# Local attention: TensorE's step put in the order of its tile shapes, one more step of pipeline depth, the token shift moved to ScalarE

## What is computed

```
for i in range(6):
    x = attn_layer(shift_tokens(x), Wqkv[i], ...) + x    # 16 heads of 64, windows of 32 tokens,
                                                         # each sees itself and the window before
    x = ffn_layer(shift_tokens(x), ...) + x              # layer norm, gated GELU, 341 hidden
shift_tokens(t): the upper half of the channels comes from the token before
attn_layer: q, k normalised per head (l2), rotary tables with a scale, scores * 8, causal mask, softmax, @ v, @ Wo
```

## Time and profile before

| | us |
|---|---|
| median of 3 runs (4217.25 to 4219.12) | 4217.94 |
| the profiled execution | 4230.46 |
| its span, first to last instruction | 4228.0 |
| one layer of local attention, first projection to first projection (1326.78 to 1905.23) | 578.45 |
| of it, end of the last step begun and MLP (1805.67 to 1905.23) | 99.56 |
| a step in the steady part | 7.605 |

### The profile page before, as it was taken

One profiled execution on the slowest core, in us unless ns is written; L12 is line 12 of the kernel. 1 busy time (PEld: TensorE's weight loads), 2 busy tenths in 40 slices (PEclk: granted clock), 3 DMA queues, 4 the chain that ended last, 5 costly groups with the idle time before them and its releaser, 6 DMA issues. The chain is left out here.

```text
span 4228.0 us, 154817 instructions
## 1 busy us (share of the span) xinstructions
PE 3986.5 (94%) x61339; PEld 2359.9 (56%) x61339; DVE 3368.7 (80%) x5724; ACT 2583.2 (61%) x5027; POOL 2537.1 (60%) x2772
## 2 busy tenths in 40 slices
PE   5888697999999999999999999999999999999998
PEld 3555486555554555545555545555455555455554
DVE  5777455899976999958999769999489997699994
ACT  4776222566665666665666656666666666566665
POOL 2111133777763777727777537777277775477771
PEclk8999998999999999999999999999999999999999
DMA  2000000000000000000000000000000000000001
GB/s 72 0 0 1 0 0 3 3 0 0 0 21 7 0 0 0 0 21 6 0 0 0 21 6 0 0 0 0 21 6 0 0 0 21 6 0 0 0 0 41
DMA packets 12340, 27.26 MB, mean 6 GB/s; under 512 B 2460, under 2 KB 6728, under 8 KB 11344
## 3 DMA queue, kind: packets, MB, share of 16 engines
q1 hardware_dynamic: 12240, 25.72, 1.7%
HBM read 23.62 MB, written 2.10 MB: 6 GB/s over the span
## 5 line engine op out<-in xcount | busy, mean ns | idle before, releaser
L954 POOL TENSOR_TENSOR w_t<-w_t 128x512 f32<-128x512 f32 x768 | 981.2, 1278 | 509.0 <-DVE w_t L1259 508.8
L1259 DVE TENSOR_TENSOR w_t<-banks,w_tab 128x512 f32<-128x512 f32 x1536 | 981.6, 681 | 46.1 <-PE banks L1130 27.7
L989 POOL TENSOR_TENSOR w_t<-w_t,w_rn 128x512 f32<-128x512 f32 x768 | 784.9, 1043 | 243.1 <-ACT w_rn L1434 243.1
L1069 PE MATMUL banks<-w_vo,w_xs 128*32 128x256 f32 x12288 | 823.2, 385 | 8.6 <-ACT w_us L1382 8.6
L1130 PE MATMUL banks<-w_qk,w_xs 128*128 128x512 f32 x1536 | 767.2, 622 | 5.8 <-issue 4.1
L1069 PEld LDWEIGHTS banks<-w_vo,w_xs 128*32 128x32 f32 x12288 | 321.7, 109 | 499.8 <-issue 368.6
L1393 ACT ACTIVATE w_pr<-w_pr 128x512 f32<-128x512 f32 x384 | 242.0, 630 | 581.8 <-DVE w_pr L1306 581.8
L1382 ACT ACTIVATE w_us<-banks 128x512 f32<-128x512 f32 x768 | 457.3, 596 | 173.1 <-PE banks L1069 173.1
L1288 DVE TENSOR_REDUCE w_ss<-w_sq 128x16 f32<-128x1024 f32 x384 | 464.3, 1209 | 0.0
L1108 PE MATMUL banks<-w_us,w_prT 128*32 128x128 f32 x10752 | 418.3, 276 | 20.7 <-issue 9.4
L981 POOL TENSOR_TENSOR w_pr<-w_pr,w_rl 128x512 f32<-128x512 f32 x384 | 403.1, 1050 | 35.0 <-DVE w_rl L1274 35.0
(11 more groups left out here) (176 smaller groups left out, 5838.2 us busy)
## 6 DMA issues: line engine op xcount, KB each, us to landing
w_qk<-w_qk_in SPq DMA_DIRECT2D x7, 1024.0 KB, 4.8
w_v<-w_v_in SPq DMA_DIRECT2D x7, 512.0 KB, 5.5
w_o<-w_o_in SPq DMA_DIRECT2D x7, 512.0 KB, 6.3
m_w<-m_w_in SPq DMA_DIRECT2D x6, 342.0 KB
xT<-x_in SPq DMA_DIRECT2D x4, 512.0 KB
out<-kept SPq DMA_DIRECT2D x8, 256.0 KB, 2.4
m_w<-m_w_in SPq DMA_DIRECT2D x6, 171.0 KB
r_tab<-r_tab_in SPq DMA_DIRECT2D x1, 512.0 KB
```

The source lines that it names most:

```text
L954: nc.gpsimd.tensor_tensor(v1, v1, v2[:, :, ::-1, :], ALU.add).then_inc(S["added"], 1)
L989: nc.gpsimd.tensor_tensor(v1, v1, rn[j % 2][:, i * HALF:(i + 1) * HALF].unsqueeze(2) .broadcast_to([P, HALF, WD]), ALU.mult).then_inc(S["n ...
L1069: last = nc.tensor.matmul(banks[WIN * g:WIN * (g + 1), 2, lo:lo + 2 * P], x[:, WIN * w:WIN * (w + 1)], wvo[:, first:first + 2, :].rearrang ...
L1259: nc.vector.tensor_tensor(dst[j % 2][:, i * C:(i + 1) * C].rearrange("p (h d) -> p h d", d=WD), src, tab[:, 2 * t + cs, i * WD:(i + 1) * W ...
```

## The change

- PE's step has a new order: projection of k, turn of q (tile n-1), projection of q, turn of k (n-1), in every second step the turned output, turn of the probabilities (now tile n-3), first half of the values, weighted values (now n-3), second half of the values, scores (n-1). All of 128*128 stand together, then all of 128*32, then the scores.
- The tile's way is one step longer: mask, maximum and subtraction are made for tile n-2 at the head of DVE's step, turn of the probabilities and weighted values for tile n-3; `LAG` is 4.
- DVE's order is: mask, maximum, subtraction (n-2); rotation of k; rotation of q; residual; sums of the squares and guard; sum of the exponentials (n-2) and reciprocal.
- ACT's order is: shift of x (new, in every second step, two copies of 64x128); square of k; copy of turned q (n-1); square of q; copy of turned k (n-1); copy of the turned probabilities (n-3); first half of the values; exponential (n-2); copy of the output; second half of the values; the two activations of the inverse norm.
- POOL's order is: edge copy (now for the tile n-2); addition for k; addition for q; multiplication by the inverse norm, twice; probabilities (n-2) times the reciprocal. It has no shift of x any more; the shifts of the first two MLP chunks are ACT's too.

The diff, cut to its core; what is left out takes away the same work from its old place or gives helpers their names:

```diff
--- before.py
+++ after.py
@@ -826,7 +826,7 @@
-    LAG = 3
+    LAG = 4
...
@@ -953,34 +941,14 @@
...
+                    if live(2) and j2 < 2:
+                        pool.wait_ge(S["u_taken"], passed(n(2) * 2))
+                        if live(4):
+                            pool.wait_ge(S["valued"], passed(n(4)))
                         pool.sem_inc(sem("gate"), 1)
+                        nc.gpsimd.tensor_copy(edge[j2][:], us[j2][:, NWIN - 1]).then_inc(S["edged"], 1)
                     if live(0):
                         add(1, "k_rotated")
...
-                    if live(2):
-                        pool.wait_ge(S["inverse"], passed(n(2)))
-                        p = pr[j % 2]
-                        nc.gpsimd.tensor_tensor(p[:], p[:], rl[j % 2][:].unsqueeze(1).unsqueeze(3)
-                                                .broadcast_to([P, 2, HALF, WIN]), ALU.mult).then_inc(S["weighted"], 1)
-                    if live(0):
                         add(0, "q_rotated")
...
@@ -988,10 +956,12 @@
...
+                    if live(2):
+                        pool.wait_ge(S["inverse"], passed(n(2)))
+                        p = pr[j % 2]
+                        nc.gpsimd.tensor_tensor(p[:], p[:], rl[j % 2][:].unsqueeze(1).unsqueeze(3)
+                                                .broadcast_to([P, 2, HALF, WIN]), ALU.mult).then_inc(S["weighted"], 1)
...
@@ -1075,21 +1061,21 @@
...
-                        pe.wait_ge(S["weighted"], passed(n(2)))
+                        pe.wait_ge(S["weighted"], passed(n(3)))
...
-                        tv, hv = j2 // 2, j2 % 2
-                        pe.wait_ge(S["p_taken"], passed(n(2)))
-                        pe.wait_ge(S["u_taken"], passed(n(2) * 2))
+                        tv, hv = j3 // 2, j3 % 2
+                        pe.wait_ge(S["p_taken"], passed(n(3)))
+                        pe.wait_ge(S["u_taken"], passed(n(3) * 2))
...
@@ -1177,13 +1116,59 @@
...
+                    if live(0):
+                        if live(1):
+                            pe.wait_ge(S["k_rotated"], passed((n(0) - 1) * 2))
...
+                        project(1)
...
+                    if live(1):
+                        if live(4):
+                            pe.wait_ge(S["p_taken"], passed(n(4)))
+                        elif not live(2):
+                            pe.wait_ge(M["residual"], finished(layer, 0))
+                        turn(0)
+                    if live(0):
+                        if live(1):
+                            pe.wait_ge(S["q_rotated"], passed((n(0) - 1) * 2))
+                        pe.sem_inc(sem("gate"), 1)
+                        project(0)
+                    if live(1):
+                        turn(1)
...
+                    if live(4) and j % 2 == 1:
+                        pe.wait_ge(S["y_taken"], passed(tiles(layer, j, seq, 4)))
+                        pe.sem_inc(sem("gate"), 1)
+                        nc.tensor.transpose(banks[:, 7, P:2 * P], ysb[:], ident[:]).then_inc(S["y_turned"], 1)
+                    if live(3):
+                        turn_probabilities()
...
+                    if live(0):
+                        values(0)
+                    if live(3):
+                        apply_probabilities()
+                    if live(0):
+                        values(1)
...
+                    if live(1):
+                        scores()
...
@@ -1261,59 +1245,56 @@
+                    if live(2):
+                        dve.wait_ge(S["scored"], passed(n(2)))
...
+                            dve.wait_ge(S["p_turned"], passed(n(4)))
...
-                        dve.wait_ge(S["qk"], passed(n(0) * 2 - 1))
+                        dve.wait_ge(S["k_squared"], passed(n(0)))
                         if live(2):
                             dve.wait_ge(S["turned"], passed(n(2) * 2))
                         rotate(1, "k_rotated")
+                        dve.wait_ge(S["q_squared"], passed(n(0)))
+                        rotate(0, "q_rotated")
...
+                    if live(4) and j % 2 == 1:
+                        dve.wait_ge(S["y_turned"], passed(tiles(layer, j, seq, 4)))
+                        lo = PAD + (j // 2) * P
+                        rows = xT[:, bass.ds(seq - 1, 1), lo:lo + P].rearrange("p b t -> p (b t)")
+                        nc.vector.tensor_tensor(rows, rows, banks[:, 7, P:2 * P], ALU.add).then_inc(S["residual"], 1)
+                    if live(0):
+                        nc.vector.tensor_reduce(ss[j % 2][:], sq[:].rearrange("p a h d -> p (a h) d"), AX, ALU.add)\
+                            .then_inc(S["sums"], 1)
+                        dve.wait_ge(S["sums"], passed(n(0)))
+                        nc.vector.tensor_scalar(ss[j % 2][:], ss[j % 2][:], 1e-24, None, ALU.max)\
+                            .then_inc(S["guarded"], 1)
                     if live(2):
                         dve.wait_ge(S["exped"], passed(n(2)))
...
@@ -1371,6 +1352,20 @@
+                def shift(t, seq):
+                    src = xT[:, bass.ds(seq, 1), :].rearrange("p b t -> p (b t)")
+                    lo = PAD + t * P
+                    for rows, back in ((slice(0, 64), 0), (slice(64, P), 1)):
+                        nc.scalar.activation(xs[t][rows, :], src[rows, lo - back:lo - back + P], ACT.Copy)\
+                            .then_inc(S[f"shifted{t}"], 1)
+
+                def shift_chunk(c):
+                    act.wait_ge(S["residual"], passed(layer * B * TILES + 2 * TILES * (c + 1)))
+                    for rows, back in ((slice(0, 64), 0), (slice(64, P), 1)):
+                        nc.scalar.activation(xm[c][rows, :].rearrange("p (b t) -> p b t", b=PER),
+                                             xT[rows, c * PER:(c + 1) * PER, PAD - back:PAD - back + T], ACT.Copy)\
+                            .then_inc(M["early"], 1)
...
@@ -1382,57 +1377,72 @@
...
+                    if live(0) and j % 2 == 0:
+                        if live(1):
+                            act.wait_ge(S["u_made"], passed(n(1) * 2))
+                        if live(STEPS):
+                            act.wait_ge(M["residual"], finished(layer, 0))
+                        if j == 0:
+                            shift(1, seq)
+                        else:
+                            shift(0, seq + 1)
+                    if tail and j < 2:
+                        shift_chunk(j)
...
+                        act.wait_ge(S["qk"], passed(n(0) * 2 - 1))
...
+                    if live(0):
+                        act.wait_ge(S["qk"], passed(n(0) * 2))
+                        nc.scalar.activation(sq[:, 0].rearrange("p h d -> p (h d)"), banks[:, 0, :], ACT.Square)\
+                            .then_inc(S["q_squared"], 1)
...
+                    if live(3):
+                        act.wait_ge(S["p_turned"], passed(n(3)))
+                        nc.scalar.activation(prT[:].rearrange("p g q -> p (g q)"), banks[:, 3, :], ACT.Copy)\
+                            .then_inc(S["p_taken"], 1)
...
+                    if live(0):
+                        values(0)
+                    if live(2):
+                        act.wait_ge(S["centred"], passed(n(2) * 2))
+                        p = pr[j2 % 2][:].rearrange("p a h r -> p (a h r)")
+                        nc.scalar.activation(p, p, ACT.Exp).then_inc(S["exped"], 1)
+                    if live(3) and j % 2 == 0:
+                        act.wait_ge(S["valued"], passed(n(3)))
+                        nc.scalar.activation(ysb[:], banks[:, 7, 0:P], ACT.Copy).then_inc(S["y_taken"], 1)
                     if live(0):
                         values(1)
+                        act.wait_ge(S["guarded"], passed(n(0)))
+                        nc.scalar.activation(lg[:], ss[j % 2][:], ACT.Ln, scale=65536.0).then_inc(S["logged"], 1)
+                        act.wait_ge(S["logged"], passed(n(0)))
+                        nc.scalar.activation(rn[j % 2][:], lg[:], ACT.Exp, scale=-0.5).then_inc(S["rnorm"], 1)
...
```

## The result

The changed kernel takes 4396.64 us (median of 4 runs, 4393.47 to 4405.15), the kernel before beside it 4218.53: a ratio of 1.0423, 95% interval 1.0405 to 1.0442. Slower, as forecast, but by 178 us instead of 100, and 6.6 us beyond the upper end of the range. The profiled executions stand at 4394.47 (span 4392.6) and 4230.46 (span 4228.0), 164.6 us of span apart.

A forecast was written before the change was run, and what follows sets the result against it. PE bound the old 7.605 us step; a chain of waits would make it 7.84. Steps 14.3 us plus end 2.3 us, times six layers, add 100 us: 4217.94 to 4318 us, range 4245 to 4390.

The forecast's parts named there:

- PE's own step, 7.05 us: In the steady steps, four of seven tile-shape changes go at 0.14 us each, leaving PE about 7.05 us of work.
- The ring: In each steady step, a chain of waits through PE, ACT and POOL back to PE sets the step at 7.84 us.
- U1 to TP: From ACT's second values copy through inverse norm and POOL's multiplications to PE's turn of the probabilities: 4.17 us.
- TP to U1: From PE's turn of the probabilities through both halves of the values to ACT's second values copy: 3.67 us.
- the term for A's wait: On PE, the weighted values wait for ACT's copy of the turned probabilities, adding 0.04 us a step.
- Where PE stands: PE idles some 0.8 us a step, mostly before the probabilities' turn and second values half; no idle before that turn refutes.
- the other path into TP: Through normalisation, turns and projection to the probabilities' turn on PE: about 1.95 us against 2.1, only some 0.15 shorter.
- DVE's chain, 7.16: DVE's own work takes 7.16 us a step, so it waits about 0.7 us for PE's scores.
- The shift on ScalarE at nothing: At the head of ACT's step in every second step, the shift copies of x cost nothing.
- The ends of the layer, 2.3 us each: One more drained step and ACT's shift copies lengthen each layer's end by 2.3 us, between 0 and 4.
- The clock. Nothing.: PE's idle time in each step doesn't lower its granted clock, so it costs nothing.
- Rival 1: In the steady steps, shape-change drains are saved and nothing replaces them; DVE's 7.16 us bounds the step: 4069 us, 10%.

The follow-up runs named there:

- e1: Changed kernel with ACT making the two inverse-norm activations ahead of the second copy of the values: 4265.62 us, 1.0087 times before.
- e9: Changed kernel with ACT's logarithm of the sums made twice in a row (useless work): 4497.78 us, one run.
- e10: Changed kernel with DVE's sum of the exponentials made twice (useless work): 4406.28 us, one run.
- g1: Changed kernel with PE's and ScalarE's steps back in the old sequence, depth and shifts kept: 4257.56 us, 1.0062 times before.
- e7: Changed kernel with DVE adding the residual between the rotations of k and q instead of behind both: 4354.81 us, one run.
- e8: Changed kernel with inverse-norm activations ahead of the second values copy, residual between the rotations, and drained steps reordered: 4151.01 us, 0.9829 times before.
- e4: Kernel before with only the per-step shift of x moved from POOL to ScalarE: 4223.23 us, one run, beside 4224.90 for the kernel before.
- g2: Changed kernel as it is, run for comparison beside the one with twelve added matmuls: 4392.83 us, 5 runs.
- g3: Changed kernel with twelve unread small matmuls in PE's stand in each layer's first drained step, repeated side by side: 4384.48 us, 5 runs.
- f5: The 4151 us kernel (inverse norm first, residual early, drained steps reordered) with two sequences in the loop body: 4548.36 us, 1.0765 times before.

## Why the prediction was wrong, and where it was right

- **PE's own step, 7.05 us.** Right: 7.04 in the steps of e1 without idle time, so 0.14 a change.
- **The ring.** Right as a mechanism: e1 breaks it, e9 lengthens it by what is put in, e10 puts three times as much beside it for nothing, g1 never closes it. Its second half, U1 to TP, was forecast at 0.49 + 0.24 + 0.30 + 1.99 + 1.15 = 4.17 and is 4.18. Its first half, TP to U1, was forecast at 3.67 and is 3.745 on the mean. **The step that failed is the term for A's wait.** I made A wait for ACT's copy of the probabilities alone (0.04 us). In every second step it waits for DVE's residual as well, a wait that stands in the code ahead of A; so the odd steps have TP to A at 1.89 and 1.73 us, the even ones 1.50. The term is 0.12 us (e7) where I had 0.04; the other terms add up to 7.80 and measure 7.805 with the residual early. That makes 7.925 for 7.84, and 0.085 x 61 x 6 is 31 us.
- **Where PE stands.** Wrong. I put 0.8 us a step of idle time mostly before TP and V1 and called its absence before TP a sign against me. PE idles 0.47 us a step and is busy 94%, not 90%, and no wait is listed at TP or V1: the waits are before the turn of q, three or four runs of matmuls ahead of TP, before the first projection of a sequence, and before A. The sign was badly chosen, since the other path into TP is nearly as long. What holds the ring shown is W's fixed 1.15 us to TP in every step, and e1 and e9.
- **Only 0.15 us to the other path into TP.** Right in size: the output's transpose, the last of that path, starts at 1617.09 and would hand over at 1617.20; TP starts at 1617.34, behind W.
- **DVE's chain, 7.16, waiting 0.7 us a step.** Right in the changed kernel: it waits 0.74, so its chain is 7.18. As the next bound it was a little too long: in e8 DVE takes 7.28 - 0.27 = 7.01 us a step.
- **The shift on ScalarE at nothing.** Right (e4).
- **The ends of the layer, 2.3 us each.** This term failed: 7.3 us were measured, 30 us in all. The sizing by ScalarE's copies rested on work that isn't on the path (the row at 1863.51). The price is the fourth drained step: 4.4 to 6.0 us (g1). That it comes from the MLP's products queueing behind its TP is read from the rows, not tested by itself.
- **"The clock. Nothing."** This step failed too. I read the steady steps and the busy share of one stretch of 6 us, in an end whose clock stayed at 1.00; the kernel before had four ends below it, and once a slowed product. The fall comes in the layer's end, behind one stand of PE; it is part of the 7.3, and 8 us of time can be had back by filling the stand (g2, g3).
- **Rival 1** lives on in e8 in part: the drains are won, though PE more than DVE is then the bound. Its 4069 us wasn't reached: 4151, since the ends grew and one step in four is 7.67.

The two terms, 31 and 30 us, are 61 of the 78 us by which the time was missed. Of the other 17, 5 are in the steps (122 us for 86, of which A's wait is 31), and the profiled executions are 164.6 us of span apart where the medians are 178 apart, 12 of these 14 because the kernel before was profiled in an execution 12 us above its median. The range held 4.0 us for a layer's end and 0.13 us more of ring; the step, 7.925, was inside it and the end, 7.3, was not.

## What to carry to other kernels

A change of order on one engine is worth its price only if no queue of another engine leads back into it: list, for every instruction that moved behind another, who waits for it and where that wait stands in its own queue, and go round until a chain meets itself one step later. List every wait in front of each link, also those that bind only in every second step. And price one more step of depth at what queues behind the last drained step, not at the work it adds.

## What the chip showed that I had not expected

- The granted clock fell behind a single stand of PE of 1.8 to 3.5 us, in most layers of one kernel and in few of another, and more work in the stand made the kernel 8 us faster.
- With a body of eight steps instructions are loaded anew in every pass, 10.7 packets of 16.4 KB, and the pass shown is about 10.8 us longer (13.07 + 8.99 + 9.44 + 8.38, less 7.67 + 7.04 + 7.23 + 7.17). The first pass of each layer isn't slowed.
- Behind 64 small score matmuls and a loop's branch PE stands 0.47 us before the next projection. Without the branch it is 0.10 us (f5). In the kernel before A stood last, and no such stand is there.
